# A fused attention layer with a gated key network: gate and key products in f16 parts, and new orders on every engine

## The reference

```
h   = LN(x);  q, k, v = h Wq, h Wk, h Wv          # 16 heads of 64
s   = q k^T / 8 + bias[clip(j - i, -16, 16)], causal
x   = x + LN(softmax(s) v  Wp + bp)
g   = LN(x);  p = g of the token before (0 at the start of a batch)
xr  = mu_r g + (1 - mu_r) p;  xk = mu_k g + (1 - mu_k) p
out = x + LN(sigmoid(xr W_r^T) * (relu(xk W_k^T)^2 W_v^T))
```

## Time and profile before

| | us |
|---|---|
| median of three runs | 2242.05 |
| lowest, highest | 2239.59, 2242.39 |
| profiled execution | 2240.61 |
| its span, first to last instruction | 2238.8 |

### The profile page before, as it was taken

How to read it: one execution, slowest core, us unless ns; L and a number is a source line. 1 busy time by engine, 2 the same in 40 slices (tenths; PEclk the granted TensorE clock), 3 DMA queues, 4 the chain that set the end, 5 groups by cost and what they waited for, 6 DMA issues and landing times. The chain is left out here.

```text
span 2238.8 us, 74837 instructions
## 1 busy us (share of the span) xinstructions
PE 2110.4 (94%) x29456; PEld 1431.2 (64%) x29456; DVE 1945.4 (87%) x5209; ACT 1686.2 (75%) x2526; POOL 1682.9 (75%) x1370
## 2 busy tenths in 40 slices
PE   2798889999999999999999999999999999999975
PEld 1355556666666667666666766666676667667664
DVE  6777778998999989998999999999999988888856
ACT  2578788877877877887778778777877877887733
POOL 1367677887888888888888888888888887777851
PEclk9899999999999999999999999999999999999998
DMA  7111112222222222332222233223222322221260
GB/s 175 34 45 49 45 42 66 61 61 71 73 62 68 69 64 61 71 72 62 68 69 65 61 70 73 64 67 69 63 61 71 73 59 66 57 55 52 70 124 22
DMA packets 336783, 147.11 MB, mean 66 GB/s; under 512 B 172976, under 2 KB 335664, under 8 KB 336432
## 3 DMA queue, kind: packets, MB, share of 16 engines
q1 hardware_dynamic: 336432, 142.33, 26.6%
HBM read 24.25 MB, written 43.06 MB: 30 GB/s over the span
## 5 line engine op out<-in xcount | busy, mean ns | idle before, releaser
L1657 POOL TENSOR_TENSOR probs<-probs_f,probs 128x1024 f16<-128x1024 f32 (+3 forms) x704 | 1121.8, 1604 | 351.2 <-ACT probs L951 348.6
L933 ACT ACTIVATE probs_f<-score_ps,score_unit 128x1024 f32<-128x1024 f32 (+3 forms) x704 | 621.2, 882 | 239.1 <-DVE score_ps L1216 113.4
L1200 DVE TENSOR_REDUCE row_max<-max_ps 128x2 f32<-128x1024 f32 (+2 forms) x640 | 632.0, 1004 | 18.6 <-PE max_ps L644 15.8
L951 ACT CAST probs<-probs_f 128x1024 f16<-128x1024 f32 (+3 forms) x704 | 566.8, 814 | 12.3
L678 PEld LDWEIGHTS misc<-v_pair,probs 128*128 128x128 f16 x4608 | 414.6, 97 | 39.7 <-issue 28.8
L678 PE MATMUL misc<-v_pair,probs 128*128 128x65 f16 x4608 | 437.7, 194 | 0.6 <-issue 0.6
L679 PE MATMUL misc<-v_pair,probs 128*128 128x64 f16 x4608 | 436.1, 193 | 0.0
L680 PE MATMUL misc<-v_pair,probs 128*128 128x65 f16 x4608 | 435.1, 193 | 0.0
L680 PEld LDWEIGHTS misc<-v_pair,probs 128*128 128x128 f16 x4608 | 417.6, 97 | 0.0
L679 PEld LDWEIGHTS misc<-v_pair,probs 128*128 128x128 f16 x4608 | 417.5, 97 | 0.0
L569 PE MATMUL misc<-xT,w_split 128*128 128x512 f16 x1536 | 370.1, 384 | 21.7 <-issue 9.4
(11 more groups left out here) (168 smaller groups left out, 3634.9 us busy)
## 6 DMA issues: line engine op xcount, KB each, us to landing
v_pair<-v_calc SPq DMA_DIRECT2D x64, 516.0 KB, 3.6
o_scratch<-o_stage SPq DMA_DIRECT2D x128, 256.0 KB, 2.4
xh<-x SPq DMA_DIRECT2D x56, 128.0 KB, 2.1
x_res<-x SPq DMA_DIRECT2D x56, 128.0 KB, 3.1
out<-out_sb SPq DMA_DIRECT2D x56, 128.0 KB, 1.7
shift_all<-shift_row SPq DMA_DIRECT2D x256, 1.0 KB
probs<-wqkv SPq DMA_DIRECT2D x1, 3072.0 KB, 13.9
probs<-band_scratch SPq DMA_DIRECT2D x8, 144.0 KB, 3.8
```

The costliest lines, as they stand in the source:

```text
L933: nc.scalar.activation(dst, score_ps[t % 2][:, :, 0:width], ACT.Exp, scale=score_unit[:]).then_inc(exp_done, 1)
L951: nc.scalar.copy(dst, src).then_inc(hi_done, 1)
L1200: last = dve.tensor_reduce(dst[:, :, i % 4:i % 4 + 1], max_ps[:, :, col:col + width], AX.X, ALU.max)
L1657: pool.tensor_tensor(low, copy_of(par + ahead, t)[:, 0:2 * width], high, ALU.subtract).then_inc(lo_done_pool, 1)
```

## The change

The gate and key products of the tail are made from f16 parts. The two weights are scaled and split in the iterations in which the output weights are; `mixed` is scaled and cast on ScalarE (`mix_high`), its low part is made on VectorE (`mix_low`), and the scales are undone in the activations behind. The orders of all engines in the loop are written anew, with new banks. The waits on the transposed heads ask for half a batch or two groups. In the beginning the bands are made unscaled and first of all; GpSimd scales both (one to bf16) once they have been read back; only 256 of 1024 columns per weight are split ahead of the first iteration, the rest at its end. The small tensors of the beginning lie inside `o_norm`. In the closing a table gives each of the 32 products one of six banks, and all orders are new; its gate and key stay in f32. Core of the diff:

```diff
-TASKS = [("o2", 1, "prev"), ("o3", 0, "prev"), ("q0", 0, "qkv"), ("ffn", 1, "ffn"), ("o0", 1, "att"),
-         ("q1", 0, "qkv"), ("v0", 1, "qkv"), ("o1", 0, "att"), ("k0", 1, "qkv"), ("k1", 0, "qkv"), ("v1", 1, "qkv"),
-         ("x2t", 0, "mix"), ("proj", 1, "proj"), ("rk", 0, "mix")]
+TASKS = [("ffn", 1, "ffn"), ("q0", 1, "qkv"), ("o2", 0, "prev"), ("o3", 0, "prev"), ("o0", 1, "att"),
+         ("v0", 0, "qkv"), ("q1", 1, "qkv"), ("o1", 0, "att"), ("x2t", 1, "mix"), ("proj", 0, "proj"),
+         ("k0", 1, "qkv"), ("k1", 0, "qkv"), ("rk", 1, "mix"), ("v1", 0, "qkv")]
+CLOSING = [("proj0", 5), ("proj1", 0), ("proj2", 4), ("proj3", 1), ("proj4", 2), ("proj5", 3), ("proj6", 2),
+           ("proj7", 3), ("x2t0", 5), ("x2t1", 1), ("x2t2", 4), ("x2t3", 5), ("rk0", 0), ("rk1", 3), ("val0", 1),
...
+        def emptied(eng, kind, j):
+            last = bank_before(f"{kind}{j}")
...
             def tail_gate_and_key(n, span):
-                pe.wait_ge(mixed_ready, 2 * KT * (n - MIX_LAG + 1))
+                pe.wait_ge(mix_lo, n - MIX_LAG + 1)
                 bank = opened("rk", n, span)
+                step = 0
                 for k in range(KT):
-                    pe.matmul(bank[:, 0:C], mixed[:, 0, k, :], wr_sb[:, k, :], start=k == 0, stop=k == KT - 1)
+                    for a, w in ((0, 0), (0, 1), (1, 0)):
+                        pe.matmul(bank[:, 0:C], mixed_parts[:, a, 0, k, :], wrk_split[:, w, 0, k, :],
+                                  start=step == 0, stop=step == 3 * KT - 1)
+                        step += 1
...
+            def mix_high(n):
+                act.wait_ge(mixed_ready, 2 * KT * (g + 1))
+                wait(act, full["rk"], g)
+                nc.scalar.activation(mixed_parts[:, 0], mixed[:], ACT.Copy, scale=mix_scale[:]).then_inc(mix_hi, 1)
...
+            def mix_low(n):
+                dve.wait_ge(mix_hi, g + 1)
+                dve.scalar_tensor_tensor(mixed_parts[:, 1], mixed[:], mix_scale[:], mixed_parts[:, 0], ALU.mult,
+                                         ALU.subtract).then_inc(mix_lo, 1)
...
+            pool.wait_ge(vec_setup, SCALES_READY)
+            pool.wait_ge(band_in, 16 * 8)
+            pool.tensor_scalar(band_bf[:], band, band_unit[:, 0:1], MASKED, ALU.mult, ALU.max).then_inc(band_scaled, 1)
+            pool.wait_ge(bandT_in, 16 * 4)
+            pool.tensor_scalar(bandT[:], bandT[:], band_unit[:, 0:1], MASKED, ALU.mult, ALU.max).then_inc(band_scaled, 1)
```

More of the change, by code:

```diff
@@ L27 @@
 VW = 2 * (D + 1) + 2 * D
[L30 removed]
+SCALES_READY, TAIL_READY = 5, 6
+FIRST = 2 * P
 RSQRT_SEED = float(0x5F3759DF) - 0.5 * (2.0 ** 31 + 2.0 ** 23)
@@ L87, in runs, with bank_before @@
     return lo <= n < hi
+def bank_before(name):
+    names = [k for k, _ in CLOSING]
+    held = [k for k in names[:names.index(name)] if CLOSING_BANK[k] == CLOSING_BANK[name]]
+    return held[-1] if held else None
 class Span:
@@ L575, in project_v @@
             def project_v(name, n, first, pairs, ring, span):
-                if span.lo == -LEAD:
-                    pe.wait_ge(split_lo, SPLIT_ORDER.index(2) + 1)
+                wait(pe, xT_in, 16 * (NB * ((n + LEAD) // NPAIR - 1) + first + 2))
+                if span.lo in (-LEAD, 0):
+                    pe.wait_ge(split_lo, SPLIT_ORDER.index(2) + (1 if span.lo else 4))
                 bank = opened(name, n, span)
@@ L728, in body @@
                     ring = (m + LEAD // 2) // (NPAIR // 2) % 2 * T
-                    if has["att"]:
-                        score(m, par, 0, 1, at)
+                    if has["ffn"]:
+                        tail_value(n, span)
                     if has["next"]:
@@ L789, in body @@
                             pe.wait_ge(vec_setup, TAIL_READY)
-                            pe.wait_ge(wp_ready, 2)
+                            pe.wait_ge(wp_ready, 4)
                         tail_project(n, par, span)
+                    if has["next"]:
+                        fill(m, par, 6, at)
+                    if has["att"]:
+                        score(m, par, 0, 9, at)
+                        score(m, par, 0, 10, at)
+                    if has["qkv"]:
+                        project_qk("k0", n, pair * P, ring, span)
+                        project_qk("k1", n, pair * P, ring, span)
+                    if has["next"]:
+                        fill(m, par, 7, at)
                     if has["att"]:
                         score(m, par, 0, 11, at)
+                    if has["mix"]:
+                        tail_gate_and_key(n, span)
                     if has["next"]:
@@ L796, in body @@
                         score(m, par, 1, 0, at)
-                    if has["mix"]:
-                        tail_gate_and_key(n, span)
+                    if has["qkv"]:
+                        project_v("v1", n, 4 * par + 2, pair // 2 * 2 * P, ring, span)
                     if has["next"]:
@@ L1428, in body @@
+                    if has["ffn"]:
+                        root_step("z", n - FFN_LAG, 2)
+                    if has["prev"]:
+                        outputs(3, m, par, 1)
+                    if has["ffn"]:
+                        root_step("z", n - FFN_LAG, 3)
+                    if has["next"]:
+                        maxima(m, par, 1, 3)
                     if has["xt"]:
                         statistics("xh", xh, n + LEAD, xh_in, 16 * (n + LEAD + 1))
-                    if has["att"]:
-                        outputs(0, m, par, 0)
+                    if has["mix"]:
+                        root_step("x2", n - MIX_LAG, 3)
@@ L1507, in body @@
-                    if has["next"]:
-                        maxima(m, par, 1, 8)
                     if has["proj"]:
```

747 lines of the change are left out of this document (416 added, 331 removed), and 3 rows, old and new, of the table CLOSING.

## The result

Both kernels ran side by side on one chip. The kernel before took 2241.36 us (2239.59 to 2242.39), the changed one 2289.5 us (2283.57 to 2294.69, 4 runs). The ratio is 1.0215, 95% interval 1.0189 to 1.0241. The change makes the kernel 48 us slower; the forecast was 36 us faster.

A forecast was written before the change was run, and what follows sets the result against it. TensorE was taken to bound the loop (32.34 us per iteration), VectorE 2.2 us behind. 2240.6 - 21.5 (loop) - 3.5 (early orders) + 1.5 (splits) - 1 (beginning) - 11 (closing) = 2205.1, stated as 2206 beside the median; range 2198 to 2214.

The forecast's parts named there:

- the price of the new VectorE operation: Low part of the mix in each loop tail, 512 elements from SBUF: 0.8 us, bounds 0.59 and 1.09.
- The sentence on the Trainium skill's rule: GpSimd and VectorE share SBUF interfaces; by that rule the new VectorE operation would cost 0.98 us, 0.18 more than taken.
- rival 2: At the seam of two iterations late VectorE results hold TensorE's in-order queue up; slower, about 2254 us; chance 0.08.
- rival 1: VectorE becomes the bound in the loop, at 32.3 us per iteration; 2226 us; chance 0.16.
- TensorE's slot: Gate and key products in each loop tail: 1.43 us instead of 1.95, so 0.52 less asked of TensorE.
- The iteration: Steady loop with the tail: 31.95 us instead of 32.34, 0.39 less, times 55 is 21.5 us gained.
- The splits of the weights: More tail weights split in the iterations that split the output weights, beside idle time: 1.5 us lost, between 0 and 3.5.
- Beginning and early orders: Start up to the first maxima: 1 us gained; reordered work in some nine early iterations: 3.5 us gained.
- Closing: From the first projection to the end: earlier loads, six banks, order by readiness; 11 us gained, bounds 0 and 18.
- The steady orders: New orders of work in the full iterations: the seam fits with 0.2 to 0.3 us to spare, costed at nothing.
- ScalarE's cast: One cast of 512 elements per iteration: 0.615 us, costed at nothing because ScalarE has 6.4 us to spare.

The follow-up runs named there:

- halves: The changed kernel with GpSimd's low part of score tile 8 made in two instructions of 512 elements; 2238.75 us.
- reduce: The changed kernel with VectorE's low part of the mix made by a reduction over one-element groups, scale and subtraction left out; 2195.63 us.
- f32gate: The changed kernel with gate and key in f32 again, without the splits of the mix and of their two weights; 2219.66 us.
- spread: The psum kernel with the splits of w_r and w_k moved one iteration later; 2209.59 us.
- psum: The changed kernel with the mixed tokens written to PSUM instead of SBUF, and their cast and low part one place earlier; 2217.22 us.
- close: The kernel before with the new closing alone; 2230.91 us.

## Why the prediction was wrong, point by point

**The step that failed** is the price of the new VectorE operation: "Ends 0.59 and 1.09, and I take 0.8, because GpSimd is busy for five sixths of an iteration". It is 2.41 us in the mean, over twice the upper end. Both rows behind the bounds were read as rates per element, of operations of 2.35 and 1.95 us; a wait for the other engine's whole instruction does not scale with the size of one's own. Even the lower end was too low: with nothing beside it the operation takes 0.72 us, not 0.59, since a part of the time does not shrink with the size. Worse, rows 4 had the sign in them: two operations of the same shape at 1730 and 2178 ns. I took their mean and their maximum for rates. In the changed kernel the first of that pair takes 1.28 us, so neither row was a time without a wait. The sentence on the Trainium skill's rule made it 0.98 for the same reason, as a tax per element; the rule says only that the two contend, and the sum from it was wrong. The orders then put the operation where GpSimd starts its longest instruction within 0.05 us, and it lost 47 of these 53 meetings. `halves` and `reduce`, and the six iterations of 31.93 us in the changed kernel itself, show that this is the cause: `reduce` differs from it in this one operation alone.

**The mechanism of the loss** is the one of rival 2: "If the gating or the low half of the mix comes late, each us costs 55". Its signs were named too: TensorE under 97% (95.2), gate and key behind VectorE, VectorE not over 96% (94.0). I gave it 0.08 and its place no price, since the price of the operation was bounded elsewhere, in rival 1. The forecast's range ended at 2236; the chance of slower was 0.08.

**TensorE's slot** was right: 1.43 predicted, 1.41 in the timeline above (1028.94 to 1030.35). So were the 18 products, 6 x 56 and 12 x 56. The gain of 0.52 us came too where nothing waits: the usual iteration is 32.45 us in `f32gate` and 31.93 in `reduce`.

**The iteration** was right where nothing is blocked: 31.95 predicted, 31.93 in the mean of `reduce`, which has an operation of 0.68 us there. The closeness is partly luck: I had VectorE even with TensorE, but in `reduce` TensorE alone sets the time (499.04 us busy of 500, VectorE 466.99). The gain was mis-sized by its base. I took one iteration of the kernel before, 32.34, for the mean; over 53 it is 32.62, because of the long ones. With an operation of 0.68 us, near the forecast price, the loop gives 53 x 0.69 = 36.6 us instead of 53 x 0.39 = 20.7. That is most of why `reduce` ends at 2195.6, below 2206.

**The splits of the weights**: 1.5 predicted, upper end 3.5. Between the second transposes of n=2 and n=4 the changed kernel takes 70.81 us (170.12 to 240.93), the one before 62.20: 8.6 lost. By `f32gate` (63.2) 7.6 of them go with the splits of w_r and w_k, the rest with the new orders. "There beside idle time" did not hold: VectorE has the four splits in one row in front of the maxima. `spread` got 4 of the `psum` version's loss back.

**Beginning and early orders**: 1 and 3.5 gained predicted. The bands are right: 8.05 and 8.02 us on GpSimd, inside 4.8 to 11, and the first maxima at 57.82. At n=2 the changed kernel was 1.7 ahead. The early orders gave nothing that can be seen: `f32gate`, without splits, stands at 389.5 in n=9, before at 389.4.

**Closing**: 11 predicted, 11.1 measured behind n=62; `close` alone gives 9.9. From the first projection to the end 71.98, within 66 to 73.

**The steady orders** were costed at nothing and give 9 us, all of it from the long iterations. I had put all their worth into the early iterations.

**ScalarE's cast**: 717 ns in place of 615, and it cost nothing, as said.

## What to carry to other kernels

Before an operation is added to VectorE, look at what GpSimd is running at that place, not at how busy it is, and price it from both sides: its own time, and its own time plus the longest instruction of GpSimd. Different durations of one shape in the trace can be the sign of such a wait, and their mean is no price. If one operand can lie in PSUM the wait is gone, but then somebody waits for the bank: count both. An operation that is faster alone can be the worse choice. And a base for a gain per iteration is taken over many iterations, since one can be 0.3 us off the mean, times 55.

## What the runs showed of the hardware

- A VectorE operation with two SBUF operands, or a scaled f32 copy within SBUF, and GpSimd's subtraction of two SBUF operands exclude each other for the whole instruction, both ways: 0.74 against 2.73 us for VectorE, 2.13 against 2.68 for GpSimd. The same pair, met 0.05 us apart in 53 iterations, went 47 times one way and 6 times the other. GpSimd operations with one input were not tried against it.
- A copy that is faster alone (0.455 us) can be the slower choice (median 2.46); the reduction form takes 0.65 to 0.69 always.
- GpSimd takes 8.05 us for 2304 elements with one input and one scalar per partition, 3.5 ns per element.
- An activation whose scale is read from memory takes longer: 467 ns for the gate's 256 elements, 383 in `f32gate` and 358 before with a constant.
- Not settled: in `psum` the gate and key wait 0.27 us for k0's low part, in `reduce`, with the low part of the mix at its later place and as long, they don't. The bank that is held longer is the likely reason, but it was not tried by itself.
